# Eight places for gathered row groups and two for counts in the last two graph layers of a GNN and FFN kernel

## The chip, the cores and the metric

The kernel is one launch on one core of one Trainium2 chip. The metric is the device time of a launch in microseconds (us). Before the change three runs gave 5639.82, 5641.1 and 5653.56 us, a median of 5641.1 us.

## What is computed

The input is a table x of 6250 nodes by 256 floats, and 106250 directed edges `src -> dst` sorted by `dst` (50000 random pairs, each in both directions, and one loop per node). Four blocks follow each other, each added to x. Cut to what matters here:

```python
x = x + L0_gnn(layernorm(x), edges, edge_weight)   # two graph layers, weighted by degrees
x = x + L0_ffn(layernorm(x))                       # two chosen experts, dense
x = x + L1_gnn(layernorm(x), edges)                # two graph layers, counts of edges
x = x + L1_ffn(layernorm(x))                       # one expert per node, capacity bound

def gcn_conv(h, W, b):                             # twice in L1_gnn
    m = (h @ W)[src] * norm[:, None]               # norm = dinv[src] * dinv[dst]
    return jax.ops.segment_sum(m, dst, num_segments=n) + b
```

## The kernel before the change, in words

Nodes are held as NT = 49 tiles of 128 rows (P = 128, D = 256 columns). The kernel calls its four graph layers 0, 1 (L0_gnn) and 2, 3 (L1_gnn). All five engines run streams written out by hand, and every dependence is a semaphore.

**A graph layer** (`sum_edges` on PE, L1161 on, and on DVE, L2272 on; `gather_edges` on POOL) walks over groups of 4 times 128 edges: 208 groups in layers 0 and 1, NGK = 132 in layers 2 and 3. For a group

- POOL issues four indirect DMAs (L834), each of which gathers 128 rows of 1 KB from a table in HBM into one of the group's four row tiles;
- DVE makes a selection matrix of 128 x 512 (`choose`, L1963), four groups ahead (AHEAD = 4);
- PE multiplies selection and rows into a PSUM bank (`product`, L1001; 4 matmuls, each shown as two instructions in fp32);
- DVE adds the bank's two halves to ACC (`add_sums`, L1990, two instructions) and counts `s_free` up: the group is summed.

Row tiles form a ring: 8 groups of places in layer 1, RK = 6 in layers 2 and 3. POOL waits before group g until group g - RK is summed. PE may be as many groups ahead of DVE as there are banks in turn (`bank_of`): 4 in layer 0, 3 in layer 1, 2 in layers 2 and 3. In the latter PE waits before the product of group g for the sum of group g - 2.

**The first 16 source tiles** (KS = 16) are not gathered edge by edge in layers 2 and 3. Their rows are loaded once per layer and multiplied by matrices of counts, in 4 units for each of the 49 tiles (196 in a layer). For unit n

- DVE makes two one-hot operands (`choose_unit`, L2253 and L2256);
- PE counts in bf16 into the single bank UNP (`count_unit`, L1130, 2 matmuls), once unit n - 1 is copied out of it;
- ACT copies the counts to SBUF (`copy_unit`, L1625) into one of three places, UNC, and waits until unit n - 3 is multiplied;
- PE multiplies counts and source rows (`sum_unit`, L1144, shown as 8 instructions).

PE's order is product(g), then perhaps early work on finished tiles, then for each unit n of group g - 1 count(n) and sum(n - 1). The units are laid over the groups by a table (MADE), 11 for every 7 groups, the first after group 4's product; so the first multiplication of source rows stands behind group 5's.

**Where things lie.** WORK is an SBUF buffer of 14912 columns. Its first 8320 are the ring of eight groups in layers 0 and 1. In layers 2 and 3 the ring takes 6240 of them, and the rows of source tiles 8 to 15 (HSX, 2048 columns) lie behind it; tiles 0 to 7 are in HSB. `load_first_rows` on SP loads each half by one DMA of 1 MB. In layer 2 the second half is issued once the last batch of the table is stored, which is also what POOL waits for; in layer 3 both halves are issued at its start, and the DMAs of the layer's own rows (L763) stand behind them.

The wait that sets the ring's depth, and the one for the source rows:

```python
                    if layer >= 2:                                          # POOL, gather_edges
                        po.wait_ge(s_free, 4 + BEGIN[2] + max(0, BEGIN[layer] - BEGIN[2] + g - RK + 1))
...
                    if layer >= 2 and g >= 2:                               # PE, sum_edges
                        pe.wait_ge(s_free, 4 + BEGIN[layer] + g - 1)
...
                if not n:                                                   # PE, sum_unit
                    pe.wait_ge(s_hsl, 32 * (i + 1))
```

## Time and profile before the change

| | us |
|---|---|
| median of three runs | 5641.1 |
| profiled execution | 5680.27 |
| its span, first to last instruction | 5678.5 |
| PE busy | 4109.1 (72%) |
| DVE busy | 3031.9 (53%) |
| POOL busy | 2965.7 (52%) |
| ACT busy | 1484.9 (26%) |

The profiled execution is 39.2 us (0.7%) above the median, and 1.8 us of it lie outside the span. Layer 1 runs from 1602 to 2999 us, layer 2 from 3391 to 4240 us and layer 3 from 4251 to 5093 us of the span. PE's instructions are pipelined and their ends are modelled. For an indirect DMA the profile's POOL row is the time in which POOL issues it, not that in which rows move.

### The profile page before, as it was taken

How to read it: one execution, taken by the hardware profiler on the slowest of the kernel's cores; microseconds unless marked ns; L12 is line 12 of the kernel's file. 1: busy time of each engine (PE TensorE's matmuls, PEld its weight loads, DVE VectorE, ACT ScalarE, POOL GpSimd, SP SyncE). 2: the span in 40 equal slices, each digit the busy share in tenths (PEclk: the TensorE clock that was granted, in tenths of full speed). 3: DMA queues.
4: the chain of work that ended last, by engine and by line, in shares of the span. 5: the costliest groups of instructions: out<-in, count | busy, mean ns of one | idle time of the engine just before them, and what ended most of it. 6: DMA issues, size and time to landing. Idle time of an engine off the chain costs nothing.

```text
span 5678.5 us, 61699 instructions
## 1 busy us (share of the span) xinstructions
PE 4109.1 (72%) x19540; PEld 3290.4 (58%) x19541; DVE 3031.9 (53%) x7908; ACT 1484.9 (26%) x4028; POOL 2965.7 (52%) x3232
## 2 busy tenths in 40 slices
PE   7765555455446576767668986888886888885999
PEld 6653433334334466656656665777765777774766
DVE  7765645455547655555555554555554554443434
ACT  6512322222222222222223322222231111124221
POOL 7736466666656555555550006655646566543232
PEclk9987777777767777777779998999998999997999
DMA  2423333333322222222221013333333332225231
GB/s 89 122 68 95 113 96 96 95 98 96 94 85 80 76 81 78 79 78 81 81 75 34 20 48 88 93 90 89 92 92 102 102 96 85 85 74 178 67 105 53
DMA packets 272028, 489.77 MB, mean 86 GB/s; under 512 B 85620, under 2 KB 176741, under 8 KB 271571
## 3 DMA queue, kind: packets, MB, share of 16 engines
q0 software_dynamic: 139312, 377.94, 23.6%
q1 hardware_dynamic: 125272, 101.03, 5.8%
q10 hardware_dynamic: 7118, 6.83, 0.4%
q8 instruction: 160, 2.62, 0.2%
q14 instruction: 166, 1.36, 0.1%
HBM read 426.41 MB, written 62.17 MB: 86 GB/s over the span
## 4 chain that ended last, share of the span: by engine, by line
PE 38%; another core or an unknown queue 25%; DVE 20%; issue 10%; ACT 3%; DVEq 2%; POOL 1%; DMA 1%; ACTq 0%; SPq 0%; POOLq 0%
PE PSA L1001 10%; PE PSA L1144 5%; PE PSA L1385 4%; DVE ACC L1990 4%; PE PSA L1371 4%; PE PSA L1272 3%; PE PSA L1288 3%; PE PSA L1152 3%; DVE XIN L1963 2%; DVE XT L1963 2%; DVE WORK L2256 1%; PE PSA L960 1%; PE PSA L966 1%; ACT ACC L1435 1%
## 5 line engine op out<-in xcount | busy, mean ns | idle before, releaser
L834 POOL DMA_INDIRECT WORK<-tab,SRC x2632 | 2521.0, 958 | 2172.0 <-issue 775.5
L1990 DVE TENSOR_TENSOR ACC<-ACC,PSA 64x256 f32 x1360 | 569.2, 419 | 1499.2 <-remote 959.1
L1001 PE MATMUL PSA<-WORK,XIN 128*128 128x256 f32 x3192 | 909.4, 438 | 281.6 <-ACT XIN L1465 202.8
L1001 PEld LDWEIGHTS PSA<-WORK,XIN 128*128 128x128 f32 x3192 | 697.2, 223 | 411.3 <-issue 293.6
L1001 PE MATMUL PSA<-WORK,XT 128*128 128x256 f32 x2072 | 596.4, 440 | 157.3 <-ACT XT L1465 124.5
L1001 PEld LDWEIGHTS PSA<-WORK,XT 128*128 128x128 f32 x2072 | 454.7, 224 | 242.4 <-issue 162.0
L1625 ACT ACTIVATE WORK<-PSA 128x512 f32<-128x512 f32 x261 | 155.8, 597 | 716.7 <-remote 373.3
L1130 PE MATMUL PSA<-WORK 128*128 128x256 bf16 x784 | 155.1, 280 | 247.7 <-ACT WORK L1625 73.0
L1152 PE MATMUL PSA<-WORK,XT 128*128 128x42 f32 x832 | 152.4, 348 | 218.7 <-DVE WORK L1963 211.9
L1963 DVE TENSOR_TENSOR XIN<-PSA,DST 128x512 f32<-128x512 f32 x412 | 279.3, 679 | 2.8 <-DVE PSA L2276 1.6
L1152 PEld LDWEIGHTS PSA<-WORK,XT 128*128 128x128 f32 x832 | 144.8, 259 | 230.2 <-DVE WORK L1963 221.9
L1144 PE MATMUL PSA<-WORK 128*128 128x256 f32 x1048 | 266.8, 401 | 0.0
L2256 DVE SCALAR_TENSOR_TENSOR WORK<-PSA,WBC 128x512 bf16<-128x512 f32 x392 | 265.5, 677 | 0.0
L1144 PE MATMUL PSA<-HSB,WORK 128*128 128x256 f32 x1040 | 259.9, 395 | 0.0
L1130 PEld LDWEIGHTS PSA<-WORK 128*128 128x128 bf16 x784 | 69.6, 103 | 312.8 <-issue 173.4
L1535 ACT ACTIVATE XIN<-XIN,HSB 128x128 f32<-128x128 f32 x504 | 159.2, 390 | 288.8 <-DVE XIN L1963 237.4
L1385 PE MATMUL PSA<-ACC,WORK 128*128 128x256 f32 (+1 forms) x1024 | 230.3, 379 | 0.0
L2632 DVE TENSOR_TENSOR WORK<-WORK,PSA 128x10 f32 x208 | 33.3, 160 | 358.3 <-remote 300.6
L1144 PEld LDWEIGHTS PSA<-WORK 128*128 128x128 f32 x1048 | 201.7, 203 | 26.9
L1458 ACT ACTIVATE DRT<-PRD,EPSD 128x4 f32<-128x4 f32 x208 | 61.6, 297 | 581.3 <-DVE PRD L2164 436.6
L1371 PE MATMUL PSA<-WORK,ACC 128*128 128x489 f32 (+1 forms) x512 | 212.9, 576 | 0.4 <-ACT WORK L1733 0.4
L1144 PEld LDWEIGHTS PSA<-HSB,WORK 128*128 128x128 f32 x1040 | 196.5, 199 | 25.4
(474 smaller groups left out, 6975.9 us busy)
## 6 DMA issues: line engine op xcount, KB each, us to landing
WORK<-tab,SRC POOLq DMA_INDIRECT x2632
ACC<-in_L_ffn_w SPq DMA_DIRECT2D x16, 1024.0 KB
tab<-WORK SPq DMA_DIRECT2D x98, 128.0 KB
slots_x<-FILL SPq DMA_DIRECT2D x4, 2080.0 KB
ACC<-slots_x SPq DMA_DIRECT2D x8, 910.0 KB
tab<-ACC SPq DMA_DIRECT2D x49, 128.0 KB
WORK<-tab SPq DMA_DIRECT2D x49, 128.0 KB
before_y<-X SPq DMA_DIRECT2D x7, 896.0 KB
```

The lines of the kernel that those rows point to most:

```text
L834: po.indirect_dma_start(out=rows[:, 0:width], out_offset=None, in_=tab[:, :], in_offset=bass.IndirectOffsetOnAxis(ap=SRC[:, c:c + 1].bitca ...
L1001: last = pe.matmul(PS[h][:, 0:D], chosen[:, j * P:(j + 1) * P], rows[:, 0:D], start=(j == 0), stop=(j == Q - 1))
L1130: last = pe.matmul(UNP[:, j * D:(j + 1) * D], low[:, j * P:(j + 1) * P], units[:, j * D:(j + 1) * D], start=True, stop=True)
L1144: last = pe.matmul(UNS[i][t % 2], UNC[i][n % 3][:, h * P:(h + 1) * P], first_rows(4 * u + h), start=(u == 0 and h == 0), stop=(u == NUN - ...
L1152: last = pe.matmul(MOVES, TO[k % 2][:, j * P:(j + 1) * P], MOVED[k // Q % 2][:, c * 2 * KX:(c + 1) * 2 * KX], start=(j == 0), stop=(j == Q ...
L1272: last = pe.matmul(PS[q % 4][:, 0:GT // 2], W1S[:, w:w + P], XT0[:, c * GT + hf * (GT // 2):c * GT + (hf + 1) * (GT // 2)], start=(c == 0) ...
L1288: last = pe.matmul(slot_o(t), H0[:, fe * GT + u * P:fe * GT + (u + 1) * P], W2S[:, fe * D:(fe + 1) * D], start=(fe == 0), stop=(fe == 2 * ...
L1371: last = pe.matmul(PS[q % 4][:, 0:hn], W1L[:, w:w + P], XT1[:, c * CAP + h0:c * CAP + h0 + hn], start=(c == 0), stop=(c == KC - 1))
L1385: last = pe.matmul(PS[BK + r % BK][0:rows, 0:D], H1[:, f * CAP + r * P:f * CAP + r * P + rows], W2L[:, (k * FC1 + f) * D:(k * FC1 + f + 1) ...
L1963: return ve.tensor_tensor(by_place(into), PLACES.rearrange("p (a n) -> p a n", a=1).to_broadcast([P, Q, P]), by_edge(places).to_broadcast( ...
L1990: return ve.tensor_tensor(rows, rows, PS[h][half, 0:D], ALU.add)
L2256: ve.scalar_tensor_tensor(UNH[i][n % 2].rearrange("p (j n) -> p j n", n=LW), PLACES_2.rearrange("p (a n) -> p a n", a=1).to_broadcast([P, ...
```

## The change

- RK is 8: the ring of layers 2 and 3 has eight groups of places, the columns that it has in layer 1.
- HSX is a list of eight tiles of 256 columns, three in XT, one in XIN and four at the end of WORK. SP loads them by eight DMAs of 128 KB (`load_more_rows`) in place of one of 1 MB; PE waits for nine DMAs a layer in place of two.
- UNC has two places a layer in place of three, and ACT's copy of unit n waits until unit n - 2 is multiplied.

```diff
-RK = 6
+RK = 8
...
-        UNC = [[WORK[:, D2 + 3 * D + 2 * k * D:D2 + 5 * D + 2 * k * D] for k in range(3)],
-               [WAX[:, 0:2 * D], WAX[:, 2 * D:4 * D], WORK[:, D3 + 3 * D:D3 + 5 * D]]]
+        UNC = [[v[:, 2 * k * D:2 * (k + 1) * D] for k in range(2)] for v in (WORK[:, D2 + 3 * D:D2 + 7 * D], WAX)]
...
-        HSX = WORK[:, RK * Q * ROW1:RK * Q * ROW1 + (KS - 8) * D]
+        HSX = [XT[:, 2 * Q * P + k * D:2 * Q * P + (k + 1) * D] for k in range(3)] + [XIN[:, 3 * Q * P:3 * Q * P + D]] \
+            + [WORK[:, D3 + (3 + k) * D:D3 + (4 + k) * D] for k in range(4)]
...
-            return HSB[:, k * D:(k + 1) * D] if k < 8 else HSX[:, (k - 8) * D:(k - 7) * D]
+            return HSB[:, k * D:(k + 1) * D] if k < 8 else HSX[k - 8]
...
-            def load_first_rows(tab, k):
-                sp.dma_start((HSB, HSX)[k][:, :].rearrange("p (t d) -> p t d", d=D),
-                             tab[8 * k * P:8 * (k + 1) * P, :].rearrange("(t p) d -> p t d", p=P)).then_inc(s_hsl, 16)
+            def load_first_rows(tab):
+                sp.dma_start(HSB[:, :].rearrange("p (t d) -> p t d", d=D),
+                             tab[0:8 * P, :].rearrange("(t p) d -> p t d", p=P)).then_inc(s_hsl, 16)
+
+            def load_more_rows(tab):
+                for k in range(8, KS):
+                    sp.dma_start(first_rows(k), tab[k * P:(k + 1) * P, :]).then_inc(s_hsl, 16)
...
-                    pe.wait_ge(s_hsl, 32 * (i + 1))
+                    pe.wait_ge(s_hsl, 16 * (KS - 7) * (i + 1))
...
-                    last = pe.matmul(UNS[i][t % 2], UNC[i][n % 3][:, h * P:(h + 1) * P], first_rows(4 * u + h),
+                    last = pe.matmul(UNS[i][t % 2], UNC[i][n % 2][:, h * P:(h + 1) * P], first_rows(4 * u + h),
...
-                if n >= 3:
-                    ac.wait_ge(s_ud, b - 2)
-                ac.activation(UNC[i][n % 3], UNP, ACT.Copy).then_inc(s_uc, 1)
+                if n >= 2:
+                    ac.wait_ge(s_ud, b - 1)
+                ac.activation(UNC[i][n % 2], UNP, ACT.Copy).then_inc(s_uc, 1)
```

SP's stream at the start of layer 2. L614 loads source rows into HSB and into HSX, L623 stores the table's last batch, L738 loads weights of layer 3's end, L645 stores tiles of the next table. Before:

```order
L614 DMA HSB<-tab 128x8x256 [waits stores_of_batch_0]
L623 DMA tab<-ACC 128x256 [waits tile_staged] x7
L614 DMA WORK<-tab 128x8x256 [waits stores_of_batch_1,stores_of_batch_0]
L738 DMA WBC<-in_L_gnn_W 128x2x256 [waits weights_loaded,windows_ready]
L645 DMA tab<-WORK 128x256 [waits tile_staged] x2
```

And with the change (L613 and L618 in place of L614):

```order
L613 DMA HSB<-tab 128x8x256 [waits stores_of_batch_0]
L626 DMA tab<-ACC 128x256 [waits tile_staged] x7
L618 DMA XT<-tab 128x256 [waits stores_of_batch_1,stores_of_batch_0]
L618 DMA XT<-tab 128x256 x2
L618 DMA XIN<-tab 128x256
L618 DMA WORK<-tab 128x256 x4
L741 DMA WBC<-in_L_gnn_W 128x2x256 [waits weights_loaded,windows_ready]
L648 DMA tab<-WORK 128x256 [waits tile_staged] x2
```

One issue has become eight at the same point of the stream; the wait ahead of them is the old one.

SP's stream at the start of layer 3, where L763 (L766 with the change) loads the layer's own rows tile by tile. Before:

```order
L656 UNCONDITIONAL_BRANCH
L614 DMA HSB<-tab 128x8x256 [waits layer_summed]
L614 DMA WORK<-tab 128x8x256
L763 DMA WORK<-tab 128x256
L763 DMA WORK<-tab 128x256 [waits own_rows_loaded] x3
```

And with the change:

```order
L659 UNCONDITIONAL_BRANCH
L613 DMA HSB<-tab 128x8x256 [waits layer_summed]
L618 DMA XT<-tab 128x256 x3
L618 DMA XIN<-tab 128x256
L618 DMA WORK<-tab 128x256 x4
L766 DMA WORK<-tab 128x256
L766 DMA WORK<-tab 128x256 [waits own_rows_loaded] x3
```

The eight loads stand ahead of the own rows. POOL's stream keeps its order in both layers; only the value of `s_free` that it waits for is smaller by two groups.

## Rows read from the trace of the kernel before

**Rows 1.** Busy time by stretch: steady parts of layers 2 and 3.

```profile
core 0: us, PE busy (x) PEld busy (x) DVE busy (x) ACT busy (x) POOL busy (x), PEclk, DMA share, GB/s
3460.00:4180.00 720.00, 622.11 (x2933) 519.02 (x2932) 394.16 (x947) 180.35 (x422) 429.52 (x454) 0.96 0.31 90
4320.00:5060.00 740.00, 627.45 (x3075) 530.12 (x3074) 382.91 (x827) 124.61 (x233) 444.04 (x470) 0.95 0.32 92
```

**Rows 2.** Waits from 3640 to 4060 us: us in total, times, longest us.

```profile
ACT WORK L1625 <- remote: 158.5, 29, 10.5
DVE ACC L1990 <- remote: 117.9, 26, 6.2
...
POOL WORK L834 <- DVE ACC L1990: 97.3, 33, 8.2
```

**Rows 3.** Groups by line, 3500 to 4180 us: busy, mean ns; idle before.

```profile
L834 POOL DMA_INDIRECT WORK<-tab,SRC x428 | 405.6, 948 | 275.8 <-DVE ACC L1990 153.4 <-issue 122.4
```

**Rows 4.** Timeline in layer 2: start us, us, what [idle before <- releaser].

```profile
3705.57 0.94 POOL L834 DMA_INDIRECT WORK<-tab,SRC  x1 [2.94 <-DVE ACC L1990]
...
3711.59 1.89 PE L1001 MATMUL PSA<-WORK,XIN 128*128 128x256 f32 x8
...
3714.32 0.95 POOL L834 DMA_INDIRECT WORK<-tab,SRC  x1 [0.30 <-issue]
3717.10 0.60 ACT L1625 ACTIVATE WORK<-PSA 128x512 f32<-128x512 f32 x1 [5.53 <-remote]
3717.19 0.85 DVE L1990 TENSOR_TENSOR ACC<-ACC,PSA 64x256 f32 x2 [3.98 <-remote]
```

**Rows 5.** Timeline of POOL at the start of layer 2.

```profile
3390.73 0.98 POOL L834 DMA_INDIRECT WORK<-tab,SRC  x1 [413.58 <-SPq L630]
...
3434.70 0.95 POOL L834 DMA_INDIRECT WORK<-tab,SRC  x1 [0.30 <-issue]
3440.61 0.94 POOL L834 DMA_INDIRECT WORK<-tab,SRC  x1 [4.96 <-DVE ACC L1990]
```

**Rows 6.** Timeline of PE at the start of layer 2.

```profile
3412.43 3.65 PE L1001 MATMUL PSA<-WORK,XT 128*128 128x256 f32 x8 [2.88 <-DMA WORK<-tab,SRC]
...
3442.33 0.61 PE L1130 MATMUL PSA<-WORK 128*128 128x256 bf16 x2 [17.69 <-DVE WORK L2256]
```

**Rows 7.** Timeline of DVE there: the sums of groups 2 and 3.

```profile
3419.89 0.85 DVE L1990 TENSOR_TENSOR ACC<-ACC,PSA 64x256 f32 x2 [13.50 <-issue]
...
3439.49 0.85 DVE L1990 TENSOR_TENSOR ACC<-ACC,PSA 64x256 f32 x2 [17.76 <-remote]
```

**Rows 8.** Busy time by stretch just before that last sum.

```profile
3438.00:3440.00 2.00, 0.00 (x0) 0.00 (x0) 0.49 (x2) 0.00 (x0) 0.00 (x0) 0.50 0.00 0
```

**Rows 9.** Timelines at the start of layer 3, POOL's and the sum of group 3.

```profile
4250.66 0.96 POOL L834 DMA_INDIRECT WORK<-tab,SRC  x1 [0.16 <-issue]
...
4298.50 0.94 POOL L834 DMA_INDIRECT WORK<-tab,SRC  x1 [3.11 <-DVE ACC L1990]
...
4297.38 0.85 DVE L1990 TENSOR_TENSOR ACC<-ACC,PSA 64x256 f32 x2 [18.20 <-remote]
```

**Rows 10.** The same of layer 1, which has eight groups of places.

```profile
1601.67 0.94 POOL L834 DMA_INDIRECT WORK<-tab,SRC  x1 [30.41 <-SPq L650]
...
1664.89 1.17 POOL L834 DMA_INDIRECT WORK<-tab,SRC  x1 [5.56 <-DVE ACC L1990]
...
1663.78 0.85 DVE L1990 TENSOR_TENSOR ACC<-ACC,PSA 64x256 f32 x2 [16.23 <-remote]
```

**Rows 11.** Timelines at the end of layer 2: POOL's last gather, and a sum behind it.

```profile
4219.64 0.95 POOL L834 DMA_INDIRECT WORK<-tab,SRC  x1 [0.30 <-issue]
...
4223.67 0.85 DVE L1990 TENSOR_TENSOR ACC<-ACC,PSA 64x256 f32 x2 [2.29 <-PE PSA L1001]
```

**Rows 12.** Timeline of SP's queue at the start of layer 2.

```profile
3385.79 3.27 SPq L623 DMA_DIRECT2D tab<-ACC  x7
3390.52 0.37 SPq L614 DMA_DIRECT2D WORK<-tab  x1
```

More of the change, by code:

```diff
@@ L329, in gnn_ffn @@
         UNH = [[WORK[:, o + D + k * D:o + D + (k + 1) * D].bitcast(bf16) for k in range(2)] for o in (D2, D3)]
-        UNC = [[WORK[:, D2 + 3 * D + 2 * k * D:D2 + 5 * D + 2 * k * D] for k in range(3)],
-               [WAX[:, 0:2 * D], WAX[:, 2 * D:4 * D], WORK[:, D3 + 3 * D:D3 + 5 * D]]]
+        UNC = [[v[:, 2 * k * D:2 * (k + 1) * D] for k in range(2)] for v in (WORK[:, D2 + 3 * D:D2 + 7 * D], WAX)]
         UNP = PS[3]
         UNS = [[PS[2][:, 0:D], PS[b][:, 0:D]] for b in (6, 5)]
-        HSX = WORK[:, RK * Q * ROW1:RK * Q * ROW1 + (KS - 8) * D]
-        assert D2 >= 11520 + D and D2 + 9 * D <= 14912 and D3 + 5 * D <= 14912
-        assert RK * Q * ROW1 + (KS - 8) * D <= RS_ * Q * ROW1
+        HSX = [XT[:, 2 * Q * P + k * D:2 * Q * P + (k + 1) * D] for k in range(3)] + [XIN[:, 3 * Q * P:3 * Q * P + D]] \
+            + [WORK[:, D3 + (3 + k) * D:D3 + (4 + k) * D] for k in range(4)]
+        assert D2 >= 11520 + D and D2 + 7 * D <= D3 + 3 * D and D3 + 7 * D <= 14912 and len(HSX) == KS - 8
         def first_rows(k):
-            return HSB[:, k * D:(k + 1) * D] if k < 8 else HSX[:, (k - 8) * D:(k - 7) * D]
+            return HSB[:, k * D:(k + 1) * D] if k < 8 else HSX[k - 8]
         W1S = WORK[:, 0:2 * KC * F0]
@@ L627, in store_table @@
                     if k == TAB3 and i == NI - 2:
-                        load_first_rows(tab3, 0)
+                        load_first_rows(tab3)
                 sp.wait_ge(s_st[0], stores_before(k, 0) + 16 * U * 4)
@@ L631, in store_table @@
                 if k == TAB3:
-                    load_first_rows(tab3, 1)
+                    load_more_rows(tab3)
             def tile_landed(k, t):
@@ L755, in _ @@
             sp.wait_ge(s_sums, 3)
-            load_first_rows(tab4, 0)
-            load_first_rows(tab4, 1)
+            load_first_rows(tab4)
+            load_more_rows(tab4)
             for t in range(NT):
```

## The prediction, written before the changed kernel ran
> **What bounds the kernel now.** The two layers that the change touches take 849 us and 842 us of 5678.5. I read busy time by stretch first [rows 1]. In the steady part of layer 2 POOL issues 454 gathers, 113.5 groups, in 720 us: 6.34 us a group. PE is busy 622.11 us, 5.48 us a group. In layer 3 it is 470 gathers, 117.5 groups, in 740 us: 6.30 us a group, with 5.34 us of PE. So PE is the busiest engine and yet idle a seventh of the time, at a granted clock of 0.95 to 0.96 (the 2.4 GHz level). Something costs 0.9 us a group that is not PE's work.
>
> The waits say what it is not [rows 2]. No wait of PE in these 420 us is for gathered rows. POOL waits 97.3 us for places, in 33 pieces, so the ring is full: rows lie ready five or six groups ahead. ACT and DVE wait 158.5 and 117.9 us for something that the profile calls remote.
>
> The timeline shows that something [rows 4]. PE's product of 3711.59 us ends by the profile at 3713.48. DVE, idle, takes it up at 3717.19, 3.7 us later, and ACT begins its copy of a count at 3717.10, after 5.53 us idle. POOL has issued without a break since 3705.57; its last gather begins at 3714.32. Then it has no place and waits, and 1.8 us after the end of that issue PE's signals arrive together. The cycle is: POOL issues two groups (10.0 us) and pauses some 2.7 us, PE's signals get through, two sums free two places. 12.7 us for two groups is the 6.34 above. Two, because PE may be only two groups ahead of the sums. The number of places does not stand in this cycle.
>
> The Trainium skill's page "Perfetto Trace Analysis" (per-instruction lifecycle, TensorE) says that a matmul's profiled end is an estimate and that the signal's way is outside the profiled window. So the trace can show that the signals are late, not why. That POOL's issuing holds them up is my reading.
>
> **The start of a layer, where depth counts.** At first the ring is empty and POOL does not pause. In layer 2 it issues from 3390.73 to 3435.65, nine groups: group 9 needs the sum of group 3 (9 - 6) [rows 5]. PE's product of group 3 ends at 3416.08 [rows 6]; its sum begins at 3439.49, 23.4 us later, when POOL has stopped and the DMA engines are idle [rows 7, 8]. PE does nothing meanwhile and takes up the first count at 3442.33. Layer 3 repeats it: first gather 4250.66, pause of 3.11 us until 4298.50, sum of group 3 at 4297.38 [rows 9]. Layer 1 has eight groups of places, and there POOL issues until group 11 lacks the sum of group 3: first gather 1601.67, pause of 5.56 us until 1664.89, sum at 1663.78 [rows 10]. From first gather to that sum it is 62.1 us with eight, 48.8 and 46.7 us with six.
>
> **The change, part by part.**
>
> 1. Two more groups of places, at the start. POOL stops before group 11 and not before group 9. It issues 8 more gathers at 948 + 300 ns (the 0.30 us of the rows) = 1.25 us: 10.0 us [rows 3, 5]. If the signal of product 3 waits for that stop, the sum of group 3 and all behind it come 10.0 us later. Bounds: 0 if the signal gets through by itself (group 2's did: its sum begins at 3419.89, amid POOL's 36 issues [rows 7]); above, layer 1's 62.1 us against 48.8 and 46.7: 13.3 and 15.4 us, though other work of that layer is in it. I take 10.0 in each layer, since in all three layers this sum came only after the stop: +20.0 us.
> 2. In the steady part: nothing, by the cycle. A full ring of eight frees a place when a full ring of six does.
> 3. At the end POOL is seven groups ahead and not five. Once it has issued its last gather, signals are prompt: a sum at 4223.67 waits for PE alone [rows 11]. Two more groups of each layer run at PE's 5.48 and 5.34 us in place of 6.34 and 6.30 [rows 1]: -1.7 and -1.9 us, -3.6 us. If nothing of it shows: 0.
> 4. The source rows by eight DMAs. SP takes 3.27 us for seven stores, 0.47 us each, so seven more issues are 3.3 us [rows 12]. The last goes out by 3394.4, and PE needs the rows 48 us later behind group 5's product, after the count at 3442.33 [rows 6]. The bytes are the same. That wait and POOL's 45 us cover it: 0. If the cover were gone, 3.3 us a layer. Behind it on SP stand weights for layer 3's end and own rows that are first used after eight groups: 0.
> 5. Counts in two places. ACT's copy of unit n now waits for product n - 2. PE does that product before count n, for which ACT waits anyway: 0. That holds as long as PE's signals arrive in their order; the two late ones of rows 4 came together. Above, each of 392 copies could wait for one more unit, but PE would have to do count n first, which its order excludes.
> 6. Operands of PE in XT, XIN and WORK, where its selections and rows already lie: 0.
>
> Sum: 20.0 - 3.6 = +16.4 us. The profiled execution of 5680.3 us would be 5696.7. Against the median of 5641.1, 39 us lower, it is **5657.5 us**, +0.29%. A measurement of this kernel tells about 0.3% (16.9 us) from no change, so that my forecast stands at the edge of what can be told, and its chance is split.
>
> **A rule that speaks the other way.** PE's idle seventh and POOL's pauses repeat at every second group. The skill's same page (Optimization Strategy) says that a gap which repeats on the engine that ought to be full can mean that SBUF or PSUM has too few buffers for the next tile. By that rule two more places would close the gap; rival A is what this would be worth here. The rows agree that POOL lacks places and disagree that PE lacks rows [rows 2].
>
> **Rivals.**
>
> - A, faster: with more places POOL no longer pauses, rows and signals flow, and a group costs PE's time. 0.86 us x 129 groups in layer 2 and 0.96 us x 129 in layer 3 are 235 us: about 5406. For it: POOL's 97.3 us of waits. Against: POOL is at 5.0 us a group already faster than the rest, so that any ring fills; and layer 1 with eight places pauses too. A weak form, in which one pause in ten goes (each 2.9 us, 120 in all), gives -35 us: 5606. Chance 0.11.
> - B, the signal gets through by itself: the late sum of group 3 is a matter of its own 23.4 us, not of POOL's stop. Then the start is unchanged and only the end gains: -3.6 us, 5637.5. For it: group 2's sum, which came with POOL issuing. Against: in layer 1 the first stop is 12.6 us later (57.7 us after the first gather, by 1664.89 - 5.56 - 1601.67, against 45.0 us), and the sum again follows it, and none comes sooner. Chance 0.22.
> - C, slower beyond the bound: in the steady cycle, on DVE's wait for PE's signal, the pause grows, since more gathers stand before the stop whenever a hiccup has emptied the ring. With some 60 pauses a layer, 120 in both, 0.1 us more for each is +12 us and 0.3 us is +36 us: 5670 to 5694. It decides from 0.01 us a pause, as the forecast is at the edge. At the upper end the pause of 2.94 us becomes layer 2's first of 4.96, +242 us; no steady row comes near that. For it: the pauses at the starts are 3.1 to 5.6 us. Against: in a full ring a stop follows every two groups, whatever the depth. Chance 0.14.
> - D, the places do nothing that can be seen, start and end cancel or are not as I read them: within 6 us of 5641. Chance 0.10.
>
> **How the numbers follow.** The forecast has 0.43. Its +16.4 us, with runs that differ by 13.8 us among three, falls above the bound in some 0.20 and below in 0.23. Slower by over 0.3%: 0.20 and C's 0.14, and 0.01 of D: 0.35. Within 0.3%: 0.23, nearly all of B (0.21) and 0.08 of D: 0.52. Faster by over 0.3%: A's 0.11 and 0.02 of B and D: 0.13. The range leaves out A and the upper half of C. Below it is B with 7 us of spread, 5630; above it is item 1's upper bound (13.3 + 15.4 - 3.6 = +25 us, 5666) and the lower half of C, 5684. The forecast's own range, from both items at their bounds, is 5641 to 5670.
>
> **What would show it.** Right: POOL's first pause in layers 2 and 3 comes 10 us later, after 44 gathers and not 36; the sum of group 3 begins 58 to 60 us after the first gather; steady parts still at 6.3 us a group; some seven sums behind POOL's last gather. Wrong: steady parts below 6.2 us a group (A) or above 6.4 (C); a sum of group 3 within 50 us of the first gather, with POOL still issuing (B). If PE is seen to wait for source rows after its first count, item 4 was wrong; if ACT's copies wait for L1144, item 5.

## The result, and the profile after

| | before | after |
|---|---|---|
| median of the comparison, 18 runs each | 5636.33 us | 5651.31 us |
| lowest and highest | 5619.91, 5653.56 | 5637.57, 5664.23 |
| profiled execution | 5680.27 us | 5643.87 us |
| its span | 5678.5 us | 5642.1 us |

The ratio of after to before is **1.0027, 95% interval [1.0017, 1.0038]**: 15 us slower, with 9.6 to 21.4 us by the interval. The forecast was +16.4 us (+0.29%), and 5657.5 us where 5651.31 us was measured.

The two profiled executions go the other way, 36 us in favour of after, and this must not be read as the change's work. Layer 1, which the change leaves alone, took 1397.6 us in the trace of before and 1362.9 us in that of after. Single executions differ by more than the change is worth, so lengths come from the medians, and a trace is good for where things stand in a layer.

Busy time of the engines over the page of after, which answers to the table of before (PE 4109.1, DVE 3031.9, ACT 1484.9, POOL 2965.7 us), and POOL's gathers and DVE's sums in the costliest groups:

```profile
PE 4107.2 (73%) x19540; PEld 3297.3 (58%) x19541; DVE 3028.6 (54%) x7908; ACT 1483.2 (26%) x4028; POOL 2966.6 (53%) x3232
...
L837 POOL DMA_INDIRECT WORK<-tab,SRC x2632 | 2522.5, 958 | 2123.5 <-issue 771.3
L1993 DVE TENSOR_TENSOR ACC<-ACC,PSA 64x256 f32 x1360 | 568.9, 418 | 1496.1 <-remote 958.7
```

The work is the same to 4 us on every engine. (After's lines stand 3 further down: L834, L1990, L1130, L1144, L1625 of before are L837, L1993, L1133, L1147, L1628.)

**The steady part** of layers 2 and 3 of after, by stretch, answers to [rows 1]:

```profile
3430.00:4150.00 720.00, 627.75 (x2988) 524.84 (x2986) 398.91 (x961) 182.66 (x430) 438.91 (x464) 0.97 0.32 92
4290.00:5020.00 730.00, 627.28 (x3039) 530.88 (x3038) 378.76 (x818) 122.71 (x230) 439.11 (x464) 0.94 0.32 92
```

464 gathers are 116 groups: 6.21 and 6.29 us a group, where it was 6.34 and 6.30. The waits of 420 us of layer 2, which answer to [rows 2]:

```profile
ACT WORK L1628 <- remote: 145.0, 28, 7.3
...
DVE ACC L1993 <- remote: 98.6, 22, 5.9
POOL WORK L837 <- DVE ACC L1993: 92.5, 35, 5.0
```

POOL still waits 92.5 us for places that a sum frees, with eight groups of them as with six (97.3). None of the three is longer than it was (158.5, 117.9 and 97.3 us).

**The start of layer 2**, timeline of POOL (start, duration, what; in brackets the idle time before and what ended it), answers to [rows 5]:

```profile
3354.20 2.38 POOL L837 DMA_INDIRECT WORK<-tab,SRC  x1 [415.08 <-SPq L633]
...
3419.55 0.95 POOL L837 DMA_INDIRECT WORK<-tab,SRC  x1 [0.30 <-issue]
3429.72 0.94 POOL L837 DMA_INDIRECT WORK<-tab,SRC  x1 [9.22 <-DVE ACC L1993]
```

The sums of groups 3, 4 and 5 in DVE's timeline there, which answer to [rows 7]:

```profile
3392.18 0.85 DVE L1993 TENSOR_TENSOR ACC<-ACC,PSA 64x256 f32 x2 [12.20 <-remote]
...
3414.58 0.85 DVE L1993 TENSOR_TENSOR ACC<-ACC,PSA 64x256 f32 x2 [19.62 <-remote]
...
3428.60 0.85 DVE L1993 TENSOR_TENSOR ACC<-ACC,PSA 64x256 f32 x2 [6.17 <-remote]
```

PE's timeline shows the counts of units 0 and 1, and the product of group 5 between them:

```profile
3395.01 0.61 PE L1133 MATMUL PSA<-WORK 128*128 128x256 bf16 x2 [9.82 <-DVE WORK L2256]
3395.41 3.62 PE L1004 MATMUL PSA<-WORK,XIN 128*128 128x256 f32 x8
3422.14 0.58 PE L1133 MATMUL PSA<-WORK 128*128 128x256 bf16 x2 [23.11 <-issue]
```

And ACT's timeline the first copy of a count:

```profile
3421.40 0.60 ACT L1628 ACTIVATE WORK<-PSA 128x512 f32<-128x512 f32 x1 [26.84 <-remote]
```

POOL issues 52 gathers without a break and stops at 3420.50. PE counts unit 0 at 3395.01, ACT copies it at 3421.40, 0.9 us after POOL's stop, and PE stood still for 23.11 us. In this layer the sums of groups 3 and 4 came while POOL was still issuing (38.8 and 61.2 us after the first gather); what was held until the stop was the count's signal, and with it everything behind. The sum of group 5 begins at 3428.60, 74.4 us after the first gather. Its product had ended at 3399.03 by the profile, 29.6 us before, and POOL had been silent for 8.1 us: a silent POOL did not bring this signal at once.

**The start of layer 3** goes as forecast; POOL's timeline, which answers to [rows 9]:

```profile
4211.87 0.96 POOL L837 DMA_INDIRECT WORK<-tab,SRC  x1 [0.16 <-issue]
...
4265.66 0.95 POOL L837 DMA_INDIRECT WORK<-tab,SRC  x1 [0.30 <-issue]
4272.70 0.94 POOL L837 DMA_INDIRECT WORK<-tab,SRC  x1 [6.09 <-DVE ACC L1993]
```

The sum of group 3 in DVE's timeline:

```profile
4271.58 0.85 DVE L1993 TENSOR_TENSOR ACC<-ACC,PSA 64x256 f32 x2 [16.75 <-remote]
```

44 gathers, then a stop, then the sum of group 3, 59.7 us after the first gather (before: 46.7).

**The end of layer 2**, POOL's last gather and the last sum in the timelines of after, answers to [rows 11]:

```profile
4170.73 0.95 POOL L837 DMA_INDIRECT WORK<-tab,SRC  x1 [0.30 <-issue]
...
4200.53 0.85 DVE L1993 TENSOR_TENSOR ACC<-ACC,PSA 64x256 f32 x2 [0.30 <-PE PSA L1004]
```

The last sum of layer 2 in the timeline of before:

```profile
4239.44 0.85 DVE L1990 TENSOR_TENSOR ACC<-ACC,PSA 64x256 f32 x2 [0.30 <-PE PSA L1001]
```

From the start of the last gather to the end of the last sum it is 30.6 us; before it was 20.7 us (4219.64 to 4240.29). Seven sums follow the last gather, where five did: POOL is two groups further ahead at the end, 2 x 5.0 us.

### The profile page after: what moved, and what is told of

It reads as the page before. It is cut to its first block, busy times and chain, and to the rows that moved or that the text cites. A ratio compares the mean times of both kernels' runs of the same rounds, so it can differ in the third digit from the quotient of the medians.

```text
span 5642.1 us, 61715 instructions
## 1 busy us (share of the span) xinstructions
PE 4107.2 (73%) x19540; PEld 3297.3 (58%) x19541; DVE 3028.6 (54%) x7908; ACT 1483.2 (26%) x4028; POOL 2966.6 (53%) x3232
## 3 DMA queue, kind: packets, MB, share of 16 engines
q0 software_dynamic: 139312, 377.94, 23.7%
## 4 chain that ended last, share of the span: by engine, by line
PE 42%; another core or an unknown queue 22%; DVE 19%; issue 10%; ACT 3%; DVEq 2%; POOL 1%; DMA 1%; ACTq 0%; SPq 0%; POOLq 0%
PE PSA L1004 11%; PE PSA L1147 7%; PE PSA L1388 4%; PE PSA L1374 4%; DVE ACC L1993 4%; PE PSA L1155 3%; PE PSA L1275 3%; PE PSA L1291 3%; DVE XIN L1966 2%; DVE XT L1966 2%; PE PSA L969 2%; PE PSA L963 1%; DVE WORK L2259 1%; PE PSA L1133 1%
## 5 line engine op out<-in xcount | busy, mean ns | idle before, releaser
L837 POOL DMA_INDIRECT WORK<-tab,SRC x2632 | 2522.5, 958 | 2123.5 <-issue 771.3
L1993 DVE TENSOR_TENSOR ACC<-ACC,PSA 64x256 f32 x1360 | 568.9, 418 | 1496.1 <-remote 958.7
L1133 PE MATMUL PSA<-WORK 128*128 128x256 bf16 x784 | 154.6, 280 | 246.2 <-DVE WORK L2259 60.0
L1628 ACT ACTIVATE WORK<-PSA 128x512 f32<-128x512 f32 x196 | 117.0, 597 | 555.5 <-remote 297.6
L1133 PEld LDWEIGHTS PSA<-WORK 128*128 128x128 bf16 x784 | 70.0, 102 | 309.6 <-issue 170.3
L1628 ACT ACTIVATE WAX<-PSA 128x512 f32<-128x512 f32 x196 | 116.9, 596 | 498.9 <-remote 233.8
L1047 PE MATMUL PSA<-WAX,ONE 1*128 1x256 f32 x98 | 52.1, 626 | 221.9 <-ACT XT L1475 192.7
L1388 PEld LDWEIGHTS PSA<-ACC,WORK 128*128 128x128 f32 (+1 forms) x1024 | 185.7, 185 | 31.4 <-issue 3.5
L1147 PE MATMUL PSA<-HSB,WAX 128*128 128x256 f32 x784 | 197.0, 397 | 0.0
```

The lines of the kernel that those rows point to most:

```text
L837: po.indirect_dma_start(out=rows[:, 0:width], out_offset=None, in_=tab[:, :], in_offset=bass.IndirectOffsetOnAxis(ap=SRC[:, c:c + 1].bitca ...
L1133: last = pe.matmul(UNP[:, j * D:(j + 1) * D], low[:, j * P:(j + 1) * P], units[:, j * D:(j + 1) * D], start=True, stop=True)
L1147: last = pe.matmul(UNS[i][t % 2], UNC[i][n % 2][:, h * P:(h + 1) * P], first_rows(4 * u + h), start=(u == 0 and h == 0), stop=(u == NUN - ...
L1388: last = pe.matmul(PS[BK + r % BK][0:rows, 0:D], H1[:, f * CAP + r * P:f * CAP + r * P + rows], W2L[:, (k * FC1 + f) * D:(k * FC1 + f + 1) ...
L1628: ac.activation(UNC[i][n % 2], UNP, ACT.Copy).then_inc(s_uc, 1)
L1993: return ve.tensor_tensor(rows, rows, PS[h][half, 0:D], ALU.add)
```

## The experiments

Twelve kernels ran. Every diff is against the changed kernel. Ratios are to the kernel before, which ran beside each of them on the same chip.

### 1. The places, the layout, and where the ring is filled

Two theories to begin with. **P**: a group of places costs some 5.0 us once, when POOL first fills it without a pause, because PE's signals are held up while POOL issues; the end of the layer gives back 0.9 us. **U**: the cost is in the rest of the change, the eight loads or the two places for counts.

`six_places_new_layout` keeps all of the change but its depth.

```diff
-RK = 8
+RK = 6
```

> The changed kernel with RK back at 6: the source rows stay in eight separate tiles with eight DMAs, the counts stay in two places. Theory P (the places alone cost: what POOL issues before its first pause delays PE's signals): as the kernel before, ratio 1.000 +- 0.001; sum of group 3 about 47 to 50 us after a layer's first gather, first pause after 36 gathers. Rival U (the eight loads or the two count places cost): ratio 1.002 to 1.003, as the changed kernel.

Measured: 5633.01 us, ratio 1.0001 [0.9989, 1.0013]. U falls: eight loads in place of one, the operands' new places and two places for counts cost nothing that can be measured. The whole of the change's time is RK.

`four_places` goes the other way.

```diff
-RK = 8
+RK = 4
```

> The changed kernel with RK = 4 in layers 2 and 3. Theory P: two places fewer than before save 2 x 5.0 us at each layer's start and lose 2 x 0.9 us at its end: -16 us, ratio 0.997; first pause after 28 gathers (group 7 needs the sum of group 3), behind POOL's last gather three sums. Rival V (rows must lie ready six groups ahead to be in time): PE waits for gathered rows in the steady parts and the ratio is 1.00 or above.

Measured: 5625.05 us, ratio 0.9981 [0.9966, 0.9995], 10.6 us less than before. The sign is P's; its 16 us lie within the interval, which runs from 2.8 to 19 us. Fewer places are faster.

`six_then_eight` starts every layer with six groups and opens the other two in its middle, at group 66, where no cold start is near.

```diff
-                        po.wait_ge(s_free, 4 + BEGIN[2] + max(0, BEGIN[layer] - BEGIN[2] + g - RK + 1))
+                        po.wait_ge(s_free, 4 + BEGIN[2] + max(0, BEGIN[layer] - BEGIN[2] + g - (6 if g < 66 else 8) + 1))
```

> Eight places, but POOL keeps six groups ahead up to group 65 and eight from group 66 on, in both layers. Theory P: what costs is that POOL issues two groups more without a pause, wherever it does: start as before (sum of group 3 at 47 to 50 us), then 10 us of late sums about group 66, and the end as in the changed kernel: ratio 1.0027, as the changed kernel. Rival S (only the first filling from an empty ring costs, with PE cold): start as before and the end's gain, -4 us: ratio 0.999 to 1.000.

Measured: 5654.9 us, ratio 1.0033 [1.0015, 1.005]. The loss is there although the start of the layer is that of six places. The trace shows where it arises. POOL's gathers from 3756.0 to 3781.2 us, at about group 66 of layer 2, by line:

```profile
L837 POOL DMA_INDIRECT WORK<-tab,SRC x20 | 18.9, 946 | 11.9 <-DVE ACC L1993 6.1 <-issue 5.8
```

The stops of POOL before and behind them, by the timeline:

```profile
3756.41 0.94 POOL L837 DMA_INDIRECT WORK<-tab,SRC  x1 [6.12 <-DVE ACC L1993]
...
3786.13 0.94 POOL L837 DMA_INDIRECT WORK<-tab,SRC  x1 [5.02 <-DVE ACC L1993]
```

And in the same 30 us, the timeline of ACT's copies, of PE's counts and of the sum that ends the stop:

```profile
3775.49 0.60 ACT L1628 ACTIVATE WORK<-PSA 128x512 f32<-128x512 f32 x1 [11.06 <-remote]
...
3776.24 0.59 PE L1133 MATMUL PSA<-WORK 128*128 128x256 bf16 x2 [8.84 <-issue]
...
3784.66 0.60 ACT L1628 ACTIVATE WORK<-PSA 128x512 f32<-128x512 f32 x1 [8.57 <-remote]
3785.01 0.85 DVE L1993 TENSOR_TENSOR ACC<-ACC,PSA 64x256 f32 x2 [8.16 <-remote]
```

POOL issues 20 gathers in a row, where in the steady part it mostly issues 8 and pauses, at times 12 or 16, and in the traces of before and `six_places_new_layout` only once 20. ACT meanwhile waits 11.06 and 8.57 us for counts, and DVE 8.16 us for a product. From the end of the sum of group 60 to that of group 80 it is 138.1 us in layer 2 and 129.9 in layer 3; the changed kernel has 123.3 and 124.1, before 123.8 and 124.9. It is the stall of the layer's start, in the middle of the layer, and it is paid when the places are filled.

`eight_then_six` starts with eight and takes two away at group 66.

```diff
-                        po.wait_ge(s_free, 4 + BEGIN[2] + max(0, BEGIN[layer] - BEGIN[2] + g - RK + 1))
+                        po.wait_ge(s_free, 4 + BEGIN[2] + max(0, BEGIN[layer] - BEGIN[2] + g - (8 if g < 66 else 6) + 1))
```

> Eight places, POOL eight groups ahead up to group 65 and six from group 66 on. Theory P: start as in the changed kernel (sums of groups 3 to 5 some 10 us late), then POOL pauses 10 us longer at group 66, where signals are prompt, and the layer ends as before: what counts is the depth at the end, ratio 1.000 to 1.001. Rival S: the start's loss stays, ratio 1.003.

Measured: 5652.18 us, ratio 1.0038 [1.0023, 1.0053]. What I wrote for P missed. I had taken for granted that a longer pause in mid-layer gives back what the fill had cost. That contradicts the prediction's own working, by which a group that runs while POOL is silent saves 0.9 us and no more: two such groups a layer give back 3.6 us in both layers together, and so does the end of the layer without this edit. By that sum the kernel should stand where the changed one stands, and it does: the intervals of 1.0038 and 1.0027 overlap. The loss is paid at the fill, and emptying the ring gives nothing back that these runs can tell.

### 2. How few places

`three_places`:

```diff
-RK = 8
+RK = 3
```

> Three groups of places in layers 2 and 3 in place of eight. Theory P (each group of places costs some 5.0 us once, when POOL first fills it without a pause, and gives back 0.9 us at the layer's end): three fewer than before in each of two layers, 2 x 3 x 4.1 = 24.6 us less than before; the step from six to four groups gave 10.6 us where the same sum said 16.4, so 16 to 25 us less is expected, a ratio of 0.9956 to 0.9972, and a first pause of POOL after 24 gathers of a layer or fewer. Theory V (PE now comes to rows that have not landed, because only two groups of rows lie ready): the steady part rises above 6.3 us for each group and the ratio is 1.000 or more; waits of PE for the row semaphores show it.

Measured: 5602.9 us against 5628.1 us, ratio 0.9946 [0.9928, 0.9963]: 30 us less than before by the ratio, above P's 16 to 25, whose upper part the interval (21 to 41 us) still holds. PE does not wait for rows in the steady part. The start of its layer 2, by POOL's timeline:

```profile
3349.52 0.98 POOL L837 DMA_INDIRECT WORK<-tab,SRC  x1 [415.06 <-SPq L633]
...
3378.88 0.94 POOL L837 DMA_INDIRECT WORK<-tab,SRC  x1 [4.43 <-DVE ACC L1993]
```

And the sum of group 2 in DVE's timeline:

```profile
3377.76 0.85 DVE L1993 TENSOR_TENSOR ACC<-ACC,PSA 64x256 f32 x2 [10.05 <-remote]
```

POOL stops after 20 gathers, at 3374.45, and the sum that it needs begins 3.3 us later.

`eight_places_wait_three` separates the number of places from how far POOL runs ahead: all eight groups of places stay, and POOL waits as if it had three.

```diff
-                        po.wait_ge(s_free, 4 + BEGIN[2] + max(0, BEGIN[layer] - BEGIN[2] + g - RK + 1))
+                        po.wait_ge(s_free, 4 + BEGIN[2] + max(0, BEGIN[layer] - BEGIN[2] + g - 3 + 1))
```

> The eight groups of places of the changed kernel, its loads and its layout are kept, and in layers 2 and 3 POOL waits before group g for the sum of group g - 3 in place of g - 8. Theory P (what costs is how many groups POOL issues ahead of the last sum without a pause, not the number or the layout of the places): the ratio is that of three places, 0.9946 (0.993 to 0.9965), about 30 us less than before, with a first pause of POOL after 24 gathers or fewer. Theory L (the places themselves cost, by where in SBUF the rows land): the ratio stays near that of the changed kernel, 1.000 to 1.003.

Measured: 5664.31 us against 5693.6 us (this chip is slower for both), ratio 0.9951 [0.9935, 0.9967]. That is the ratio of three places. One constant in the changed kernel's wait turns 0.3% slower into 0.5% faster; the places themselves cost nothing.

`two_places`:

```diff
-RK = 8
+RK = 2
```

> Two groups of places in layers 2 and 3. Theory P alone goes on: another 2 x 5 us less than three places (ratio 0.9946), 0.993. Theory V (rows late) has its price here if anywhere: a sum, four gathers of 0.96 us, a landing of some 2 us, 14 or more us of products for two groups of which only one is ready: the steady part rises from 6.27 us for each group to 6.5 or more, 130 x 0.23 x 2 = 60 us or more, a ratio of 1.004 or more. V is taken as the likelier for two places.

Measured: 5672.8 us, ratio 0.997 [0.9953, 0.9988]: still faster than six, and above the 0.9946 and 0.9951 of the two kernels with three, so that neither theory hit it. PE's weight loads for the products by line over 720 us of layer 2 (busy, mean ns; idle before and what ended it), with two places:

```profile
L1004 PEld LDWEIGHTS PSA<-WORK,XIN 128*128 128x128 f32 x544 | 103.3, 194 | 49.2 <-DMA WORK<-tab,SRC 33.4 <-issue 1.9
```

With three places:

```profile
L1004 PEld LDWEIGHTS PSA<-WORK,XIN 128*128 128x128 f32 x552 | 107.0, 194 | 15.4
```

With two, PE waits 33.4 us for gathered rows here; with three, no wait for rows is large enough to be named. Three gives the lowest ratio; that two is slower than three is not fully shown, as the intervals overlap.

What a group of places costs when it is filled stands in the traces. Us from a layer's first gather to the end of the sum of group 12 (the 13th pair of rows of DVE's `add_sums` in the layer), when every kernel is past its start:

| kernel | groups that POOL may be ahead | layer 2 | layer 3 |
|---|---|---|---|
| after | 8 | 117.1 | 117.4 |
| before | 6 | 106.1 | 105.4 |
| `six_places_new_layout` | 6 | 105.2 | 103.9 |
| `four_places` | 4 | 94.1 | 93.3 |
| `three_places` | 3 | 86.9 | 87.7 |
| `eight_places_wait_three` | 3 | 88.4 | 90.0 |
| `two_places` | 2 | 84.8 | 85.8 |

Each has one trace, but from eight down to three every step is there in both layers, at 5 to 7 us a group down to four and 3 to 7 us from four to three. From three to two it is 2 to 4 us.

### 3. The same in layer 1

Layer 1 has eight groups of places in both kernels. `four_places_layers_1_to_3` and `three_places_layers_1_to_3` let POOL run only four or three groups ahead in it as well.

```diff
-RK = 8
+RK = 4
...
+                    elif layer == 1:
+                        po.wait_ge(s_free, 4 + BEGIN[1] + max(0, g - 3))
                     elif m >= RS_:
```

> Four groups of places in layers 2 and 3, and in layer 1 POOL waits for the sum of the group four behind in place of eight (its places stay eight). Theory P holds in layer 1 too, whose sum of group 12 comes 115 us after its first gather where layers 2 and 3 with four groups show 93 to 94 us: four groups fewer filled without a pause are 4 x 4.1 = 16 us less, or 10 us by the share that the step from six to four gave; with the 10.6 us of four places alone 21 to 27 us less than before, a ratio of 0.9952 to 0.9963. Rival: layer 1 ends on VectorE's masks (PE's matmuls of L1155 wait for DVE L1966), so that what POOL's start saves is waited for again: the ratio stays that of four places alone, 0.998, or layer 1 gets longer, since the rows then land late (0.999 or more).

Measured: 5597.95 us, ratio 0.9942 [0.9926, 0.9959], 33 us less than before by the ratio. Against four places alone (0.9981) layer 1 gave another 0.0039; from its first gather to the end of the sum of group 12 it took 92.8 us where before took 115.2. Its rival, that layer 1 hangs on VectorE's masks and returns nothing, falls. The other one has RK = 3 and `g - 2`:

```diff
-RK = 8
+RK = 3
...
+                    elif layer == 1:
+                        po.wait_ge(s_free, 4 + BEGIN[1] + max(0, g - 2))
                     elif m >= RS_:
```

> Three groups of places in layers 2 and 3, and in layer 1 POOL waits for the sum of the group three behind. From the runs of four (0.9981), three (0.9946) and four with layer 1 (0.9942): layer 1's wait at four gave 0.0039, and the step from four to three gave 0.0035 for two layers, 0.0017 for one; three in all three layers is then 0.9946 - 0.0039 - 0.0017 = 0.989 by theory P, with the sum of group 12 of layer 1 some 87 us after its first gather in place of 93. Rival: the gains overlap (chance between runs, or layer 1 waits for rows at three), ratio 0.992 to 0.995.

Measured: 5661.85 us against 5693.6 us, ratio 0.9939 [0.9917, 0.9961]. The sum of all gains, 0.989, fell. The gain at layer 1's start is there (86.6 us to the end of the sum of group 12, about as expected), so the rest of the run did not keep it; why, no run shows. It is the lowest ratio among the kernels that compute the reference, but it cannot be told from 0.9942 and 0.9946; the three did not all run on one chip.

### 4. What holds up the signals

**H**: POOL's issuing, whatever it issues. **T**: the traffic of the rows. `sp_rows_layer3` has six groups of places and lets SP load the rows of layer 3 with plain transfers. It leaves out the gather by edge number in that layer: each transfer takes 128 consecutive rows. SP loads the layer's own rows in between, from group 13 on.

```diff
-RK = 8
+RK = 6
...
+            for g in range(NGK):
+                sp.wait_ge(s_free, 4 + BEGIN[2] + max(0, BEGIN[3] - BEGIN[2] + g - RK + 1))
+                for k, rows in enumerate(rows_of(3, g)):
+                    r = (4 * g + k) % NT * P
+                    sp.dma_start(rows[:, 0:D], tab4[r:r + P, :]).then_inc(s_plain[slot_of(3, g)], 16)
...
-            gather_edges(3, tab4, D)
```

> Six groups of places. The rows of layer 3 are loaded by SP, as 528 plain transfers of 128 consecutive rows each, with the same bytes in the same places; this leaves out the gather of layer 3's rows by their edge numbers, so the sums of layer 3 are of other rows. POOL issues nothing in layer 3. Theory H (PE's signals are held up by POOL's issuing of gathers): layer 3 runs at PE's own pace of 5.3 to 5.5 us for each group in place of 6.3, the sum of a group follows its last matmul by well under 1 us from the start on, and the ratio to the kernel before is about 0.98 (132 groups x 0.8 to 1.0 us and some 20 us at the start and the end, 105 to 150 us less). Theory T (the rows' own traffic or their landing sets the pace, whoever issues it): layer 3 stays at 6.3 us for each group, and the ratio is 0.997 to 1.003.

Measured: 5439.54 us against 5628.1 us, ratio 0.966 [0.9643, 0.9678]: 190 us less, and more than H said. Busy time by stretch, 540 us of layer 3 of `six_places_new_layout`:

```profile
4270.00:4810.00 540.00, 465.43 (x2237) 393.30 (x2236) 286.80 (x620) 90.76 (x170) 326.11 (x345) 0.94 0.33 95
```

The same of this kernel:

```profile
4260.00:4800.00 540.00, 540.00 (x2813) 470.28 (x2813) 349.51 (x750) 112.87 (x214) 0.00 (x0) 1.00 0.39 116
```

PE is busy for the whole of it at a granted clock of 1.00, and does 2813 matmuls in place of 2237. The DMA engines moved more than before, 116 GB/s in place of 95, so the amount of traffic does not set the pace: T falls. All waits over 100 us between 4300 and 4800 us:

```profile
ACT WAX L1638 <- PE PSA L1143: 286.2, 123, 3.7
DVE ACC L2003 <- PE PSA L1014: 174.0, 85, 3.6
ACT WORK L1714 <- PE PSA L1033: 107.7, 33, 3.3
```

Nothing here waits on "remote" any more; ACT and DVE wait for PE alone.

I would have stopped at H. `pool_plain_rows_layer3` is its control: the same transfers, issued by POOL.

```diff
-RK = 8
+RK = 6
...
+                    if layer == 3:
+                        for k, rows in enumerate(rows_of(3, g)):
+                            r = (4 * g + k) % NT * P
+                            po.dma_start(rows[:, 0:D], tab4[r:r + P, :]).then_inc(landed, 16)
+                        continue
```

> Six groups of places. The control of the run in which SP loaded layer 3's rows: the same plain transfers of 128 consecutive rows (which leaves out the gather of layer 3's rows by edge), but issued by POOL. Theory H (it is POOL's issuing that holds up PE's signals, whatever rows it names): layer 3 keeps waits on 'remote' and some 6 us for each group as long as POOL's issue of a transfer takes about 1 us, and the ratio is near that of six places, 0.99 to 1.00; if a plain transfer costs POOL less than the gather's 0.95 us, layer 3 shortens by as much. Theory R (scattered rows or the indirect form were the cause, and consecutive rows took it away): layer 3 falls to 5.0 to 5.1 us for each group as with SP, and the ratio is 0.966 to 0.970.

Measured: 5488.54 us against 5685.59 us, ratio 0.9649 [0.9627, 0.9672]. H falls in the form in which I had put it. POOL's transfers by line over the whole execution:

```profile
L838 POOL DMA_DIRECT2D WORK<-tab x528 | 280.7, 541 | 350.2 <-DVE ACC L1998 338.7 <-issue 11.5
```

Its first burst in layer 3 by the timeline:

```profile
4250.88 12.90 POOL L838 DMA_DIRECT2D WORK<-tab  x24
4263.98 10.60 POOL L838 DMA_DIRECT2D WORK<-tab  x20 [0.21 <-issue]
```

Busy time by stretch, 540 us of layer 3:

```profile
4300.00:4840.00 540.00, 540.00 (x2818) 470.33 (x2817) 350.12 (x752) 113.37 (x215) 228.83 (x431) 1.00 0.39 116
```

A plain transfer costs POOL 541 ns with no gap behind it, the gather 948 and 300 ns. But the difference is not how long POOL issues: in the first 23.7 us of layer 3 it issues 44 transfers with one gap of 0.21 us, and the sums in that time come on PE's heel. DVE's timeline:

```profile
4262.84 0.85 DVE L1998 TENSOR_TENSOR ACC<-ACC,PSA 64x256 f32 x2 [11.26 <-PE PSA L1009]
...
4264.56 0.85 DVE L1998 TENSOR_TENSOR ACC<-ACC,PSA 64x256 f32 x2 [0.24 <-PE PSA L1009]
...
4266.51 0.85 DVE L1998 TENSOR_TENSOR ACC<-ACC,PSA 64x256 f32 x2 [0.49 <-PE PSA L1009]
```

The queue is not the difference either. POOL's plain transfers and its gathers move on the same one, in packets of one mean size (2.7 KB). By DMA queue, this kernel from 4300 to 4840 us, and `six_places_new_layout` from 4270 to 4810 us:

```profile
q0 software_dynamic: 20551, 56.15, 34.7%
```

```profile
q0 software_dynamic: 16533, 45.19, 29.1%
```

So what holds up PE's signals goes with the gathers: with their indirect form, or with the scattered rows that they fetch. The Trainium skill's page "DMA: Bandwidth & Descriptors" (SWDGE vs HWDGE vs iDMA) gives irregular transfers to GpSimd and its software path and plain ones to the hardware path of SP and ACT. For the hold-up that choice made no difference here: the plain transfers ran on the software queue from POOL (0.9649) and on a hardware queue from SP (62.31 MB on `q1 hardware_dynamic` from 4260 to 4800 us of its trace; 0.966). No run here gathers by edge number in another way than by POOL's indirect transfers, so the 190 us are a price, and no kernel here takes them with the reference computed.

`gather_consecutive_rows_layer3` was to tell the form from the scatter: indirect gathers by POOL in layer 3, by indices that name the consecutive rows of the two runs before. It leaves out the gather by edge number in the same way.

```diff
-RK = 8
+RK = 6
...
-                        c = Q * g + k
+                        c = Q * g + k if layer < 3 else (Q * g + k) % NT
...
+            po.iota(SRC[:, 0:NT], pattern=[[P, NT]], base=0, channel_multiplier=1)
             po.iota(NIDI.bitcast(i32), pattern=[[P, NT]], base=0, channel_multiplier=1).then_inc(s_nid, 1)
             po.iota(E8I.bitcast(i32), pattern=[[0, NT], [1, E1]], base=0, channel_multiplier=0).then_inc(s_nid, 1)
+            po.wait_ge(s_nid, 2)
             gather_edges(3, tab4, D)
```

> Six groups of places. Layer 3's rows are gathered by POOL's indirect transfers as before, but by indices that name 128 consecutive rows, the same rows as in the two runs with plain transfers (which leaves out the gather of layer 3's rows by edge). Plain transfers by SP and by POOL both gave 5.0 us for each group and 0.966 and 0.965, so that POOL as the issuer is not the cause. Theory I (the indirect form: POOL's work for a gather, 0.95 + 0.30 us with no gap): layer 3 keeps 6.3 us for each group and its waits on 'remote'; ratio 0.999 to 1.001, that of six places. Theory R (scattered rows, by what they ask of HBM and the DMA engines): layer 3 falls to 5.0 to 5.1 us for each group and the ratio is 0.966 to 0.970.

Measured: 4742.05 us against **4741.34 us for the kernel before**, ratio 1.0002 [0.9993, 1.0011]. In this comparison the unchanged kernel before took 4736.04 to 4748.09 us in all its 15 runs, where in every earlier comparison its median was 5628 to 5694 us. The trace is of the new kernel. Busy time by stretch, 500 us of its layer 2, which is gathered by edge number as always:

```profile
2850.00:3350.00 500.00, 500.00 (x2500) 430.21 (x2499) 337.29 (x811) 155.49 (x365) 378.69 (x399) 1.00 0.40 114
```

All waits over 100 us in these 500 us:

```profile
ACT WORK L1630 <- PE PSA L1135: 312.7, 152, 4.4
DVE ACC L1995 <- PE PSA L1006: 156.3, 70, 4.1
POOL WORK L837 <- issue: 119.2, 391, 0.3
```

And DVE's sums among the page's costliest groups, of the whole execution:

```profile
L1995 DVE TENSOR_TENSOR ACC<-ACC,PSA 64x256 f32 x1360 | 569.2, 419 | 631.2 <-PE PSA L1006 604.3
```

Where after's sums wait 1496.1 us, 958.7 of them on "remote", these wait 631.2 us, 604.3 of them for PE's product itself. No wait of this execution is put down to "remote", in any layer, scattered rows or not. POOL issues 399 gathers in 500 us, 5.01 us a group, with 0.3 us between them and no pauses, and PE is never idle. The run therefore says nothing on form or scatter; it says that the hold-up needs something more than unbroken gathers, which was there in all the other comparisons and absent in this one.

## Why the prediction was right, and where it was not

**Item 1, two more groups cost 10.0 us a layer at the start: the size held, a little low.** POOL's first stop came 21.4 us later in layer 2 (66.3 us after the first gather, where it was 44.9) and 10.0 us later in layer 3. From the first gather to the end of the sum of group 12 the traces have 117.1 and 117.4 us, where before had 106.1 and 105.4: +11.0 and +12.0 us (+11.9 and +13.5 against `six_places_new_layout`). What the text said would be held, the sum of group 3, was held in layer 3, at 59.7 us, within the 58 to 60 foretold. In layer 2 it was not: it ended 3393.03 - 3354.20 = 38.8 us after the first gather with POOL still issuing, which was the sign named for rival B. What B then claims, an unchanged start, did not follow, because the next signals were held in its place, until 52 gathers were out. The step that failed is "this sum": in layer 2 it was the signal of the first count that came with the stop, and which signal is held changes from run to run. It is also not true that all comes with the stop: the sum of group 5 came 8.1 us behind it. One reading of the rows was off as well: between the product of group 3 and its late sum PE did not do nothing, it ran the product of group 4 (3420.88 to 3424.63 us of before) and then stood still for the 17.69 us of [rows 6].

**Item 2, nothing in the steady part: right.** 6.21 and 6.29 us a group, against 6.34 and 6.30. `six_places_new_layout` has 6.26 in the stretch shown above (345 gathers, 86.25 groups, in 540 us) and 6.22 in layer 2 (437 gathers in 680 us), and even three places keep the pace (457 and 459 gathers in 720 us, 6.30 and 6.27 us a group). Rival C (a longer pause) needed above 6.4, rival A (the pauses vanish) below 6.2, and neither came. The page "Perfetto Trace Analysis" of the Trainium skill (Optimization Strategy), by which a repeating gap can mean too few buffers, does not hold here for the buffers of rows in SBUF: the gap repeats with eight, six, four and three groups of places, and the ratios are 1.0027, 1, 0.9981 and 0.9946. The same passage of the Trainium skill names PSUM too, and more PSUM banks for PE's sums were not tried.

**Item 3, -3.6 us at the layers' ends: neither shown nor refuted.** The longer end is there, 30.6 us behind the last gather in place of 20.7. The traces lean to more than 3.6: from the end of the sum of group 80 to that of the last sum, layers 2 and 3 together, it is 610.7 us after, 620.8 before and 618.5 in `six_places_new_layout`. Single traces differ by as much. Its worth is below what the medians tell: `eight_then_six`, which gives the depth up earlier, stands at 1.0038 with an interval that holds 1.0027. If these traces are right, items 1 and 3 were both too small, with opposite signs, and that the sum of +16.4 us came so near the measured 15 us is in part luck. The forecast's own range, too, was added up wrongly: with both items at their bounds it begins at 5637.5 us (5641.1 - 3.6) and not at 5641.

**Items 4, 5 and 6, nothing for the loads, the counts' places and the operands: right,** by 1.0001 [0.9989, 1.0013] for all three together. The interval alone would just hold item 4 without its cover (6.6 us, 1.0012), but the trace of after shows the cover: PE takes up the first source rows at 3422.52 us, 0.4 us behind the start of its count, and waits for none of them.

**The reading under it all** was that POOL's issuing holds up PE's signals. The forecast needed only that the signal which blocks the rest comes when POOL stops, and at the starts in the traces above it did, 0.9 to 5.0 us behind the stop; the next one, in layer 2 of after, did not (8.1 us, with the DMA engines at rest in the row 3422 to 3426 below). As a cause it was too wide. Plain transfers by POOL held up nothing, and in one comparison the gathers did not either. And the hold-up was undersized: the prediction had put it at 0.9 us a group, the 6.3 less PE's own 5.34 to 5.48. Without it a group takes 5.0 us (431 transfers, 107.75 groups, in 540 us of `pool_plain_rows_layer3`, with PE busy throughout), since PE's own busy time shrinks too. One part of that is the clock. Busy time by stretch of after, PE's stall at the start of layer 2, the first 4 us behind it, and 10 us later:

```profile
3395.00:3422.00 27.00, 4.02 (x10) 2.70 (x10) 3.40 (x8) 0.60 (x2) 19.40 (x21) 0.50 0.37 106
3422.00:3426.00 4.00, 3.86 (x10) 2.68 (x10) 0.42 (x1) 0.39 (x1) 0.00 (x0) 0.50 0.00 0
3436.00:3440.00 4.00, 4.00 (x22) 3.43 (x21) 3.94 (x10) 1.43 (x3) 2.45 (x3) 1.00 0.16 44
```

PE's granted clock is 0.50 (the 1.2 GHz level) in and right behind the stall and 1.00 (2.4 GHz) later; 10 matmuls fit into 4 us, then 22. The 0.94 to 0.97 of the steady stretches are means over such pieces; in after it is 0.50 from 3612 to 3615 us, for one.

**P's line for fewer places**, 4.1 us for each group and layer, says 16 us from six to four and 8 from four to three; 10.6 and about 20 were measured (the 20 from two comparisons, 0.0035 with an interval of about 0.0023, 13 us, to either side). The two misses have opposite signs and lie within the intervals. P's sums for eight, four and three places, ratios of 1.0029, 0.9971 and 0.9956, all lie within the measured intervals. That each step has the sign that it says is shown from eight down to three.

## What to carry to other kernels

Depth is not free even where nothing waits for the memory: an engine that runs ahead does its work at a time when it may be in the way of others, so ask how far ahead the consumer really needs it, and try the wait alone (one constant) before making room for more places. Where a fixed amount of run-ahead is paid once at each fill, count the fills: per layer here, not per group. And before a cause is believed because taking the suspect away helped, keep the suspect and change only the form of its work: here SP's transfers made POOL look guilty, and the same transfers by POOL cleared it of all but the gathers. And put the unchanged kernel into every comparison: without it the 4742.05 us of the last run would have passed for a gain of 16%.

## What the runs showed of the hardware

- **PE's signals come late while POOL gathers without a break.** In layer 2 of after ACT's first copy starts 25.8 us behind the profiled end of the count, and the sum of group 5 29.6 us behind that of its product, shown as "remote"; they begin 0.9 and 8.1 us after POOL's stop. With plain transfers in a layer the same signals arrive at once, and the layer gains some 190 us of 842.
- **The hold-up can be absent altogether.** One comparison of six had none of it: the kernel before took 4741.34 us, 16% less than its 5641.1 us, with DVE's, ACT's and POOL's busy times unchanged (3027.3, 1481.5 and 2972.0 us on the page of that comparison's profiled kernel). What differs there, the runs do not say; it ran on the chip numbered 5, and so had, 40 minutes earlier, a comparison in which before took 5628.1 us. In its layer 2 POOL hardly waits for places, and 5.01 us a group is what four gathers take it, 4 x (0.95 + 0.30). So the price of depth found here is not to be carried over; no kernel with another depth than six ran in it.
- **A plain transfer of 128 rows of 1 KB costs POOL 541 ns, a gather of as many rows 948 ns and 300 ns of gap.**

**What stays open:** whether the indirect form or the scattered rows hold up the signals (the run that was to tell fell into the undisturbed comparison), by what path they do, why a signal can be late with POOL and the DMA engines at rest, and what the undisturbed comparison lacked. Whether the hold-up could be avoided by a third place for PE's sums, so that PE could be further ahead of DVE, was not tried: all eight PSUM banks are in use in layers 2 and 3.
